# A graph network on one core: five units of the sorted list per step in place of four

## What is computed

```python
h = relu(layernorm(x))
f = shifted_softplus(edge_attr @ W1 + b1) @ W2 + b2
x = x + segment_sum(h[dst] * f, src)                 # the filter layer
h = relu(layernorm(x))
x = x + rgcn_conv(relu(rgcn_conv(h, ...)), ...)      # mean by type, two times
```

## Time and profile before

| | us |
|---|---|
| median of 3 runs | 7132.72 |
| the profiled execution, its own time | 7149.41 |
| its span, first to last instruction | 7147.6 |
| `prepare` | 0 to 155 |
| plain groups | 155 to 1469 |
| accumulating groups | 1469 to 2712 |
| `make_table` | 2712 to 2935 |
| two convolutions | 2935 to 7148 |

### The profile page before, as it was taken

How to read it: one execution, slowest core, us unless ns; L and a number is a source line. 1 busy time by engine, 2 the same in 40 slices (tenths; PEclk the granted TensorE clock), 3 DMA queues, 4 the chain that set the end, 5 groups by cost and what they waited for, 6 DMA issues and landing times. The chain is left out here.

```text
span 7147.6 us, 113836 instructions
## 1 busy us (share of the span) xinstructions
PE 4359.0 (61%) x28573; PEld 3531.3 (49%) x28573; DVE 3819.8 (53%) x11981; ACT 2911.5 (41%) x7788; POOL 5383.4 (75%) x5304
## 2 busy tenths in 40 slices
PE   2888888888888887645555555555444444444444
PEld 1666666667777773444444444444333333333333
DVE  8888888868777877645555555555211111111111
ACT  2666666654444446523333333333222222222222
POOL 6777777778888885577777777777677777777777
PEclk6999999999999998756666666666555555555555
DMA  3766666589998988634444443333222222222222
GB/s 107 188 183 182 181 181 162 149 173 190 188 189 186 192 166 273 209 89 104 106 106 106 105 105 105 106 105 103 67 55 56 56 56 56 56 56 56 56 56 54
DMA packets 688258, 879.21 MB, mean 123 GB/s; under 512 B 132110, under 2 KB 512426, under 8 KB 687277
## 3 DMA queue, kind: packets, MB, share of 16 engines
q1 hardware_dynamic: 446088, 530.23, 26.9%
q0 software_dynamic: 238864, 340.26, 21.9%
q10 hardware_dynamic: 2634, 1.21, 0.1%
HBM read 615.41 MB, written 255.76 MB: 122 GB/s over the span
## 5 line engine op out<-in xcount | busy, mean ns | idle before, releaser
L1907 POOL DMA_INDIRECT got<-table_dram,cidx x3322 | 3154.0, 949 | 1057.3 <-issue 996.9
L1956 PE MATMUL bank<-got,share 128*128 128x128 f32 x6656 | 1632.7, 422 | 1856.0 <-DMA got<-table_dram,cidx 1855.5
L1956 PEld LDWEIGHTS bank<-got,share 128*128 128x128 f32 x6656 | 1400.6, 311 | 2010.3 <-DMA got<-table_dram,cidx 2009.7
L1536 POOL DMA_INDIRECT msg_dram<-total,idx x1008 | 986.7, 979 | 335.3 <-issue 281.1
L2010 ACT ACTIVATE share<-cto_node,etcol 128x128 f32<-128x128 bf16 x3328 | 1071.1, 393 | 354.0 <-DVE cto_node L2101 318.4
L1551 POOL DMA_INDIRECT acc_dram<-total,idx x653 | 1035.7, 1586 | 206.5 <-issue 194.6
L2000 ACT ACTIVATE cidx<-srccol 128x4 int32<-128x4 f32 x832 | 169.5, 205 | 2395.2 <-PE bank L1956 2381.6
L303 DVE SCALAR_TENSOR_TENSOR xs<-bank,mask_hi,xs 128x128 f32 x416 | 146.2, 351 | 1690.0 <-PE bank L1956 1690.0
L1129 PEld LDWEIGHTS bank<-w,soft 128*128 128x128 f32 x3328 | 446.1, 195 | 56.7 <-issue 41.5
L1129 PE MATMUL bank<-w,soft 128*128 128x128 f32 x3328 | 447.1, 278 | 0.0
L1120 PE MATMUL bank<-edges_t,w 128*128 128x512 f32 x832 | 428.9, 597 | 2.4 <-DVE soft L1360 2.4
(11 more groups left out here) (262 smaller groups left out, 7877.8 us busy)
## 6 DMA issues: line engine op xcount, KB each, us to landing
edges<-in_edge_attr SPq DMA_DIRECT2D x415, 256.0 KB
unit<-msg_dram SPq DMA_DIRECT2D x616, 129.0 KB
clow<-rows_dram SPq DMA_DIRECT2D x416, 128.0 KB
got<-table_dram,cidx POOLq DMA_INDIRECT x3322
table_dram<-made SPq DMA_DIRECT2D x98, 512.0 KB, 5.0
table_dram<-umade SPq DMA_DIRECT2D x98, 512.0 KB, 3.0
low<-rows_dram SPq DMA_DIRECT2D x164, 256.0 KB
win<-split_dram SPq DMA_DIRECT2D x416, 96.0 KB
```

What stands on the lines that cost most here:

```text
L1536: pool.indirect_dma_start(g.msg_dram[:, :], bass.IndirectOffsetOnAxis(ap=idx[k][:, j:j + 1], axis=0), total[k][:, j, :], None).then_inc(s_ ...
L1907: pool.indirect_dma_start(got[k][:, j, :], None, g.table_dram[which][:, :], bass.IndirectOffsetOnAxis(ap=idx[k][:, j:j + 1], axis=0)).then ...
L1956: ins = nc.tensor.matmul(window[k], share[k][:, j, :], got[ka][:, j, :], start=j == 0, stop=j == TG - 1)
```

## The change

Five units go in a step in place of four. The division of the groups follows from it: 272 plain groups and 144 accumulating ones; 544 + 126 = 670 units in 134 steps. To fit in SBUF and PSUM, the unit buffers go from four to three, the split buffers of `prepare` from four to three (NSP, NH), and the first of the five sums stands in the free columns of bank 6, behind the duplicate sums that ACT copies. So PE's units now also wait for that copy (`s_totc`), and its duplicate sums for the first add. The four one-hots, one instruction each, become a small add (`key`) and one comparison over all five units, placed behind the counts. `prepare` counts 9 slabs in place of 8 and broadcasts the block numbers through two banks.

```diff
-UNITS = 4
+UNITS = 5
@@ prepare
-    NSP = 4
-    NH = 4
+    NSP = 3
+    NH = 3
@@ filter_layer
-    NU = 4
+    NU = 3
...
-        reduced = [bank_r[:, m * P:(m + 1) * P] for m in range(UNITS)]
+        reduced = [bank_c[1][:, HALF * (F + 1):HALF * (F + 1) + P]] + [bank_r[:, m * P:(m + 1) * P] for m in range(UNITS - 1)]
@@ PE, duplicate sums
                         need(pe, s_totc, s.at(3))
+                        if windows.own and s.live(UNIT_LAG + 3, NA + g.NSET, NA):
+                            need(pe, s_added, b.at(UNIT_LAG + 3) * UNITS + 1)
@@ PE, units
                         need(pe, s_added, b.at(lag) * UNITS)
+                        need(pe, s_totc, s.at(3) + 1)
@@ DVE
                         add_unit(b, 3)
+                        add_unit(b, 4)
...
-                        for m in range(UNITS):
-                            ins = v.scalar_tensor_tensor(unit_hot[b.slot(2, lag)][:, m, :, :],
-                                                         unit[b.slot(NU, lag)][:, m, :, F:F + 1].to_broadcast([P, UNIT // P, P]),
-                                                         so.unit_off[:, bass.ds(b.at(lag) * UNITS + m, 1)],
-                                                         so.iota_f[:, :].unsqueeze(1).to_broadcast([P, UNIT // P, P]),
-                                                         ALU.add, ALU.is_equal)
-                        ins.then_inc(s_unit_hot, 1)
+                        need(dve, s_unit_hot, b.at(lag))
+                        v.tensor_tensor(key[:, :, :, 0], unit[b.slot(NU, lag)][:, :, :, F],
+                                        so.unit_off[:, bass.ds(b.at(lag) * UNITS, UNITS)].unsqueeze(2).to_broadcast([P, UNITS, UNIT // P]),
+                                        ALU.add).then_inc(s_key, 1)
@@ DVE, behind the counts
+                        v.tensor_tensor(unit_hot[b.slot(2, lag)][:, :, :, :].rearrange("p m k q -> p (m k) q"),
+                                        key[:, :, :, 0].rearrange("p m k -> p (m k)").unsqueeze(2).to_broadcast([P, UNITS * (UNIT // P), P]),
+                                        so.iota_f[:, :].unsqueeze(1).to_broadcast([P, UNITS * (UNIT // P), P]),
+                                        ALU.is_equal).then_inc(s_unit_hot, 1)
```

More of the change, by code:

```diff
@@ L148, in __init__ @@
         self.NFIX = self.NU - self.NMAIN
-        assert self.NBX <= self.NFIX <= P and self.NMAIN <= 512 and self.NA >= 16
+        assert self.NBX <= self.NFIX <= P and 512 < self.NMAIN <= 1024 and self.NA >= 16
         self.acc_dram = [nc.dram_tensor(f"acc_dram{j}", [self.NACC, F], F32).ap() for j in range(TG)]
@@ L350, in prepare @@
         idf = [ids[k].bitcast(F32) for k in range(3)]
-        spare = sb("spare", [P, max(EQ, g.NT)], I32)
+        spare = sb("spare", [P, max(EQ, g.NT, 2 * g.NTA)], I32)
         idt = spare[0:QP, 0:EQ]
@@ L370, in prepare @@
         scaled = sb("scaled", [F, F])
-        digits = [wide[1][:, 0:EQ // 2].bitcast(BF16)[:, k * NTA:(k + 1) * NTA] for k in range(2)]
+        digits = [wide[1][:, 0:EQ // 2].bitcast(BF16)[:, 0:NTA], sb("low_digit", [P, NTA], BF16)[:, :]]
         pick = wide[1][:, EQ // 2:].bitcast(F32)
@@ L605, in _ @@
             pe.wait_ge(s_binned, len(slabs) + 3)
-            nc.tensor.matmul(g.bank[7][:, 0:NMAIN], g.ones3[:, :], ended, start=True, stop=True).then_inc(s_counted, 1)
+            nc.tensor.matmul(g.bank[3][:, 0:NMAIN - 512], g.ones3[:, :], ended[:, 512:], start=True, stop=True)
+            nc.tensor.matmul(g.bank[7][:, :], g.ones3[:, :], ended[:, 0:512], start=True, stop=True).then_inc(s_counted, 1)
         @block.vector
@@ L779, in main_units @@
                 dve.wait_ge(s_counted, len(slabs) + 3)
-                chain(v.tensor_copy(so.unit_blk[:, 0:NMAIN], g.bank[7][:, 0:NMAIN]))
-                chain(v.tensor_scalar(so.unit_off[:, 0:NMAIN], g.bank[7][:, 0:NMAIN], -float(P), None, ALU.mult))
+                for blocks, c0, c1 in ((g.bank[7], 0, 512), (g.bank[3], 512, NMAIN)):
+                    chain(v.tensor_copy(so.unit_blk[:, c0:c1], blocks[:, 0:c1 - c0]))
+                    chain(v.tensor_scalar(so.unit_off[:, c0:c1], blocks[:, 0:c1 - c0], -float(P), None, ALU.mult))
             def duplicates():
@@ L914, in filter_layer @@
         edges = [sb(f"edges{k}", [P, TG, F]) for k in range(NE)]
-        rows = [sb(f"rows{k}", [2, GE], BF16) for k in range(NE)]
         low = [sb(f"low{k}", [P, 2, GE], BF16) for k in range(NE)]
@@ L922, in filter_layer @@
         chunk_split = pieces[2].bitcast(BF16)[:, 0:CB * 3 * F].rearrange("p (b k f) -> p b k f", k=3, f=F)
+        rows = [unit[2][0:2, :, :, :].rearrange("p m k f -> p (m k f)").bitcast(BF16)[:, k * GE:(k + 1) * GE] for k in range(NE)]
         place = sb("place", [P, TG])
@@ L945, in filter_layer @@
         counts = bank_s[:, 0:R]
-        reduced = [bank_r[:, m * P:(m + 1) * P] for m in range(UNITS)]
+        reduced = [bank_c[1][:, HALF * (F + 1):HALF * (F + 1) + P]] + [bank_r[:, m * P:(m + 1) * P] for m in range(UNITS - 1)]
+        key = sb("key", [P, UNITS, UNIT // P, 1])
         ranks = g.bank[6][:, 0:NBX]
@@ L956, in filter_layer @@
         s_unit_hot = sem("f_unit_hot")
+        s_key = sem("f_key")
         s_red = sem("f_red")
@@ L1468, in step @@
                                         ALU.max).then_inc(s_idx, 1)
-                    if windows.own and s.live(UNIT_LAG + 1, NA + g.NSET, NA):
+                    keyed = windows.own and s.live(UNIT_LAG + 1, NA + g.NSET, NA)
+                    if keyed:
                         lag = UNIT_LAG + 1
@@ L1503, in step @@
                         add_window(nc, dve, g, g.cnt, counts, s_pass, s_cnt, s.at(2), s.at(2))
+                    if keyed:
+                        lag = UNIT_LAG + 1
+                        need(dve, s_key, b.at(lag) + 1)
+                        v.tensor_tensor(unit_hot[b.slot(2, lag)][:, :, :, :].rearrange("p m k q -> p (m k) q"),
+                                        key[:, :, :, 0].rearrange("p m k -> p (m k)").unsqueeze(2).to_broadcast([P, UNITS * (UNIT // P), P]),
+                                        so.iota_f[:, :].unsqueeze(1).to_broadcast([P, UNITS * (UNIT // P), P]),
+                                        ALU.is_equal).then_inc(s_unit_hot, 1)
                 if not windows.own:
```

## The result

The changed kernel takes 7231.19 us (median; 7227.91 to 7242.14), the kernel before 7134.52 us in the runs beside it: a ratio of 1.0138, 95% interval 1.0125 to 1.015. It is slower by 96.7 us, where 98 were forecast.

What follows compares the result with a forecast made beforehand. The prediction took POOL's scatters, 7.57 us an accumulating step, to bound the kernel before. Its terms, 102.7 - 1.0 - 2 + 12.4 - 14 = +98 us on the median of 7132.7, gave 7231 us, range 7160 to 7290.

Steps and rivals of the forecast that it cites:

- The term that decides: Accumulating steps: with three unit buffers `edges` lands later, its two-step loop takes 17.44 us, 8.7 us a step.
- first rival: Accumulating steps: `edges` lands in 2.7 us as with empty queues, 8.2 us a step, 7165 us; chance 0.11.
- the choke: Rival, DMA engines: five unit loads make `edges` land in 5 us or later, 9.3 us a step, 7310 us; chance 0.09.
- The one over the adds: Loop from soft to soft over DVE's adds and PE's units: grows from 6.60 to 7.83 us a step.
- The buffer wait doesn't bite: Rival: the adds' loop and SP's queue are left, together some 7.95 us a step, 7133 us; chance 0.09.
- The plain steps: Filter layer: 20 groups become plain, at 5.135 us each, +102.7 us.
- The intervals: Between units on PE: 133 of 8.7 us, 1157.1 against 1158.1 us before, -1.0 us.
- `prepare`: Opening stage: waits for buffers 9.0 us, ninth slab 2.2, wider rows and broadcasts 1.2; +12.4 us.
- the end: POOL's finish behind the last units on PE: 16.4 us in place of 31, -14 us.
- The one-hots are nothing either way: DVE: four operations, 1.68 us a step, become one of 1.3 to 1.7 us; no effect on the time.
- POOL stays the bound, 7096 us: Rival, accumulating steps: fifth add hidden, loads land in time, a step stays at 7.57 us, kernel faster; chance 0.07.
- hidden as long as ACT doesn't wait for a scatter: PE's units wait for ACT's 0.7 us copy of the duplicate sums, covered by 2.3 us of soft and two adds.

Runs made afterwards that it cites:

- `edges` ahead: The changed kernel with SP issuing the load of `edges` one step earlier, in front of the unit loads: 7147.21 us.
- first three groups: Groups of follow-up runs, each on a chip of its own, where the kernel before takes 7133.76, 7135.61 and 7135.92 us.
- the two kernels with `edges` ahead on SP: The changed kernel with SP issuing `edges` a step earlier, 7147.21 us, and that with the fourth add also ahead of soft, 7165.93 us.
- the adds apart: The changed kernel with the fourth of five adds moved ahead of soft on DVE, only the fifth behind it: 7202.04 us.

## Why the prediction was right, and where its terms were off

**The term that decides was right by its own mechanism.** Three unit buffers put `edges` behind five unit loads in a loop of two steps: 8.73 us against 8.7. Its pieces in the timeline: 0.74 to the first load (0.9), 4.75 to `edges` (4.8), 3.84 for landing and handover (3.75), 5.66 to the units (5.50), 2.47 (2.49). The 3.7 for the landing was a choice between two rows of the plain groups, 2.73 and 4.14, so that it came out this near is in part luck. One issue moved ahead took 83 of the 97 us away, one moved behind added 196, and the buffer alone, with four units, cost 7. The early landing of the first rival (8.2 us a step) didn't come, nor did the choke. PE's waits for `edges` are smaller than forecast, 67.3 us in 119 steps, 0.57 a step in place of some 0.7.

**The loops below it.** The one over the adds is 7.81 (7.83 forecast) where nothing else holds it and 7.92 in the changed kernel's short steps; SP's queue, with `edges` ahead, is busy (1040 - 20.4) / (1040 / 8.01) = 7.85 us a step (7.83). The third was mis-sized: the prediction left POOL at 7.57, and with this one-hot it is 7.9 to 8.0. "The buffer wait doesn't bite" gave 7133 for this state; with `edges` ahead it was 7147.

**The plain steps.** Forecast +102.7; from first to last plain scatter it is 1385.9 against 1292.7, +93.2, since this execution ran at 1.275 us a scatter, not 1.284. The same groups took 1392.7 with `edges` ahead (182.4 to 1575.1), so some 7 us of it are between executions.

**The intervals, `prepare`, the end.** 1160.8 us against 1158.1, +2.7 (-1.0 forecast, and -2 more for the last two steps); `prepare` +10.5 (+12.4), the waits for buffers 7.3 in place of 9.0; why they are less no run shows. (The four places that the prediction names and the 1.1 add up to 8.9.) POOL ends at 2803.5, 18.2 behind the last units, in place of 31: -12.5 (-14). The units' start after the last plain scatter came 2.8 later. At POOL's end the sum is 10.0 + 93.2 + 2.8 + 2.7 - 12.5 = +96.2, and the medians differ by 96.7. That 98 came so near is luck: the terms are off by -9.5 us for the plain steps, +5.7 for the intervals, +1.5 for the end, -2.4 for the start of the plain groups, and +2.8 for a start that nobody priced, and these cancel. The spans of the two profiled executions differ by only 82.6, since behind POOL's end that of before took 13.6 us longer; its own time stood 16.7 above its median.

**Two steps were wrong and cost nothing here.** "The one-hots are nothing either way" holds for DVE's time, but the comparison holds POOL's scatters, 0.44 us a step; it would have cost had POOL stayed the bound, so "POOL stays the bound, 7096 us" wasn't to be had with this one-hot. I weighed only DVE's time. And the new wait on PE, called "hidden as long as ACT doesn't wait for a scatter", is hidden only because the kernel is slow: at 8.06 us a step it was 136.5 us of 1040, though taking it out gave just 0.11 us a step, since POOL was full. To put the first sum in another bank was not tried.

**Left open:** a time for the best version on the chips of the first three groups; the 19 us between the two kernels with `edges` ahead on SP; and whether SP's queue, by itself, would hold the steps at 7.85, for which `edges` ahead on SP would have to be run with five one-hots. No run has five units with four buffers; what the third buffer does is read from the kernel before with three and from the moved issues.

## What to carry to other kernels

When a unit of work is added to a step and its buffers get fewer for it, follow a load that stands behind the buffer's wait in the same queue: here not the units but `edges`, an innocent load of the next step, became late, and its two-step loop set the time. Price a longer operation also by what it excludes: a DVE operation with two SBUF inputs should be short where POOL issues all the time. Removing one loop shows the next only a few per cent below (8.73, then three side by side at 7.8 to 8.0, then 7.65), so a fix is worth the distance to the next loop and not its own wait. Before one queue is named as the lock, look at what every other engine waits for: POOL was full here while hardly anybody waited for it.

## What the runs showed of the hardware that was not expected

A scatter issued during a DVE comparison of 1.48 us ends 1.42 to 1.43 us after the comparison, and took 1.98, 2.33 and 2.83 us in three places in place of 1.55.

After idle times of 1.74 and 3.24 us PE worked at half its clock for a few microseconds: 20 matmuls took 4.10 in place of 2.47 us, four transposes 1.12 in place of 0.60. The length of the wait doesn't decide it: in the changed kernel 20 matmuls took 4.10 us behind a wait of 1.80 (at 2290.16) and 2.47 behind one of 1.73 (at 2517.74), and with the adds apart four transposes took 0.66 behind a wait of 3.00 (at 2314.92).

On another chip the kernel before took 8426.54 us. Where it is the same program, in the kernel with the comparison alone, the plain scatters run from 171.9 to 2068.4 there, 1896.5 us against 1292.7, at a granted clock of 0.81; most of the rest lies behind the filter layer. What makes that chip slower these runs don't show.
